# Turning sorted token tiles two at a time in the middle stage of a mixture-of-experts kernel

## The reference, cut to what matters

```python
rw = _gating(hidden_states, sim_matrix, gates)          # weights of the 16 experts, all but 1 or 2 of them 0
q = jnp.einsum('btc,ech,bte->bth', hidden_states, q_proj, rw)
k = jnp.einsum('btc,ech,bte->bth', hidden_states, k_proj, rw)
v = jnp.einsum('btc,ech,bte->bth', hidden_states, v_proj, rw)
scores = jnp.einsum('bqh,bkh->bqk', q, k) * scale        # then causal softmax over 128 tokens, ao = attn @ v
out = jnp.einsum('bth,ehc,bte->btc', ao, o_proj, rw)
```

## Time and profile before

| | |
|---|---|
| median of 3 runs | 1060.92 us (1060.51 to 1061.6) |
| profiled execution: span from first to last instruction | 1060.5 us |
| PE busy | 964.6 us, 91% of the span |
| DVE, ACT, POOL busy | 872.8, 581.5, 680.9 us |
| DMA | 137.72 MB, mean 130 GB/s |

### The profile page before, as it was taken

How to read it: one execution, slowest core, us unless ns; L and a number is a source line. 1 busy time by engine, 2 the same in 40 slices (tenths; PEclk the granted TensorE clock), 3 DMA queues, 4 the chain that set the end, 5 groups by cost and what they waited for, 6 DMA issues and landing times.

```text
span 1060.5 us, 23609 instructions
## 1 busy us (share of the span) xinstructions
PE 964.6 (91%) x6830; PEld 889.4 (84%) x6830; DVE 872.8 (82%) x2884; ACT 581.5 (55%) x1569; POOL 680.9 (64%) x896
## 2 busy tenths in 40 slices
PE   4999999999999639999999599999999999999998
PEld 3778887887788528999999499999999999998997
DVE  4799999999999747555555399999999999999998
ACT  4666666666666305444444355655555556555554
POOL 5447777777776683000000588888888888888885
PEclk9999999999999859999999699999999999999999
DMA  2123344443333257888886332333333233333231
GB/s 65 52 72 125 122 143 150 150 135 123 124 124 101 95 189 233 285 277 256 254 266 226 111 90 87 100 97 90 90 100 98 85 93 100 84 93 100 83 93 36
DMA packets 106308, 137.72 MB, mean 130 GB/s; under 512 B 13762, under 2 KB 93634, under 8 KB 106180
## 3 DMA queue, kind: packets, MB, share of 16 engines
q1 hardware_dynamic: 87348, 83.98, 25.2%
q0 software_dynamic: 17408, 50.35, 16.1%
q10 hardware_dynamic: 1424, 1.84, 0.5%
HBM read 70.06 MB, written 66.06 MB: 128 GB/s over the span
## 4 chain that ended last, share of the span: by engine, by line
DVE 44%; PE 36%; issue 10%; POOL 5%; ACT 2%; DMA 2%; SPq 1%; POOLq 0%; DVEq 0%; ACTq 0%
PE bank L1383 10%; PE bank L1385 9%; PE bank L1384 9%; DVE w_attn L1366 6%; DVE x L1320 4%; DVE qk_e L1320 4%; PE bank L1390 4%; DVE phi L1072 3%; DVE row_x L1360 3%; DVE attn L1084 2%; DVE kvm L1105 2%; POOL sorted_x L694 2%; DVE stats L1112 2%; DVE stats L957 2%; DVE zden L1081 1%
## 5 line engine op out<-in xcount | busy, mean ns | idle before, releaser
L1383 PE MATMUL bank<-wo_hi,split_lo 128*128 128x256 f32 x1024 | 304.8, 298 | 9.9 <-DVE x L1320 4.4
L1385 PE MATMUL bank<-wo_hi,split_hi 128*128 128x256 f32 x1024 | 289.0, 282 | 0.0
L1384 PE MATMUL bank<-wo_lo,split_hi 128*128 128x256 f32 x1024 | 288.7, 282 | 0.0
L1383 PEld LDWEIGHTS bank<-wo_hi,split_lo 128*128 128x128 f32 x1024 | 194.1, 190 | 23.1 <-DVE x L1320 11.3
L1384 PEld LDWEIGHTS bank<-wo_lo,split_hi 128*128 128x128 f32 x1024 | 194.3, 190 | 0.0
L1385 PEld LDWEIGHTS bank<-wo_hi,split_hi 128*128 128x128 f32 x1024 | 193.7, 189 | 0.0
L890 ACT ACTIVATE h<-bank,rwo 128x256 f32<-128x256 f32 x256 | 107.3, 470 | 117.9 <-PE bank L1385 113.9
L767 POOL DMA_INDIRECT row_y<-sorted_y,pair_now x128 | 124.2, 970 | 31.8 <-issue 18.3
L760 POOL COPY pair_now<-pair_at 128x2 uint32<-128x2 uint32 x64 | 16.0, 249 | 178.3 <-SPq L567 178.3
L1221 DVE TENSOR_TENSOR split_lo<-bank,split_hi 128x256 fp32r<-128x256 f32 x144 | 61.0, 424 | 69.1 <-ACT split_hi L852 67.8
L1320 DVE SCALAR_TENSOR_TENSOR x<-bank,rwo,x 128x256 f32<-128x256 f32 x256 | 108.5, 473 | 2.2 <-PE bank L1385 1.8
(11 more groups left out here) (215 smaller groups left out, 2630.5 us busy)
## 6 DMA issues: line engine op xcount, KB each, us to landing
sorted_y<-row_y SPq DMA_DIRECT2D x36, 384.0 KB, 3.2
sorted_y<-w_attn SPq DMA_DIRECT2D x36, 384.0 KB, 3.1
row_x<-sorted_x SPq DMA_DIRECT2D x72, 128.0 KB, 2.9
h_rows<-h SPq DMA_DIRECT2D x64, 128.0 KB, 1.7
row_x<-h_rows SPq DMA_DIRECT2D x64, 128.0 KB, 2.3
out_h<-row_x SPq DMA_DIRECT2D x64, 128.0 KB, 1.7
phi<-sorted_x SPq DMA_DIRECT2D x36, 128.0 KB, 3.0
qk_neg<-sorted_x SPq DMA_DIRECT2D x36, 128.0 KB, 3.1
```

The source lines that it names most:

```text
L1383: pe.matmul(ps, left[1][c], right[0][c], start=(c == 0), stop=False)
L1384: pe.matmul(ps, left[0][c], right[1][c], start=False, stop=False)
L1385: last = pe.matmul(ps, left[0][c], right[0][c], start=False, stop=(c == n - 1))
```

## The change

The turns, hi and lo of the middle stage are done for two tiles at once, at the even steps. Four transposes fill a whole PSUM bank of 512 columns, and hi and lo are one operation of 512 columns each. The eight split tensors become two large ones, so that the slots of two tiles lie next to each other. The products, the copies out, the loads and the stores stay operations of one tile (the stores of two), in their old order. The semaphores pair_turned, pair_hi and pair_lo count pairs of tiles in place of tiles; PE waits for the loads of both tiles ahead of the four transposes, and ACT, ahead of hi, for the product of the last tile that used the slots.

```diff
-        split = [[sb(f"split_{n}{q}", [P, CH, P], F32R) for n in ("hi", "lo")] for q in range(4)]
+        split_all = [sb(f"split_{n}", [P, 4, CH, P], F32R) for n in ("hi", "lo")]
+        split = [[w[:, q, :, :] for w in split_all] for q in range(4)]
+        split_pair = [[w[:, 2 * n:2 * n + 2, :, :].rearrange("p q c t -> p (q c t)") for w in split_all]
+                      for n in range(2)]
...
+        def after_two(eng, step, tile):
+
+            if tile.c >= 0:
+                eng.wait_ge(done[step], tile.c // 2 + 1)
...
-                        after(sp, "pair_turned", tile.shift(-8))
+                        after_two(sp, "pair_turned", tile.shift(-8))
...
-                    tile = i.shift(2)
-                    if tile.inside(PAIR_TILES):
-                        after(act, "pair_product", tile.shift(-4))
-                        after(act, "pair_turned", tile)
-                        act.copy(split[tile.q][0][:, :, :].rearrange("p c t -> p (c t)"),
-                                 ps_turn[tile.p][:, 0:C]).then_inc(done["pair_hi"], 1)
+                    first = i.shift(2)
+                    if first.inside(PAIR_TILES) and not first.p:
+                        after(act, "pair_product", first.shift(-3))
+                        after_two(act, "pair_turned", first)
+                        act.copy(split_pair[first.q // 2][0], ps_turn[first.q // 2][:, :]).then_inc(done["pair_hi"], 1)
...
-                    tile = i.shift(2)
-                    if tile.inside(PAIR_TILES):
-                        after(dve, "pair_hi", tile)
-                        hi, lo = [w[:, :, :].rearrange("p c t -> p (c t)") for w in split[tile.q]]
-                        dve.tensor_tensor(lo, ps_turn[tile.p][:, 0:C], hi.bitcast(F32), ALU.subtract
+                    first = i.shift(2)
+                    if first.inside(PAIR_TILES) and not first.p:
+                        after_two(dve, "pair_hi", first)
+                        hi, lo = split_pair[first.q // 2]
+                        dve.tensor_tensor(lo, ps_turn[first.q // 2][:, :], hi.bitcast(F32), ALU.subtract
...
-                    tile = i.shift(2)
-                    if tile.inside(PAIR_TILES):
-                        after(pe, "pair_lo", tile.shift(-2))
-                        pe.wait_ge(pair_loaded[tile.c % 8], tile.eighth * 16 + 16)
-                        turn(ps_turn[tile.p], *halves(x_buf[tile.c % 8])).then_inc(done["pair_turned"], 1)
+                    first = i.shift(2)
+                    if first.inside(PAIR_TILES) and not first.p:
+                        after_two(pe, "pair_lo", first.shift(-4))
+                        for tile in (first, first.shift(1)):
+                            pe.wait_ge(pair_loaded[tile.c % 8], tile.eighth * 16 + 16)
+                        turn(ps_turn[first.q // 2], *halves(x_buf[first.c % 8]), *halves(x_buf[first.c % 8 + 1])
+                             ).then_inc(done["pair_turned"], 1)
                     if i.inside(PAIR_TILES):
                         e = experts[i.q]
                         after(pe, "pair_copied", i.shift(-4))
-                        after(pe, "pair_lo", i)
+                        after_two(pe, "pair_lo", i)
```

## The result

The changed kernel takes 1062.70 us, the median of 20 runs, against 1061.04 us for the kernel before (20 runs): ratio 1.0017, 95% interval 1.0010 to 1.0023, 1.1 to 2.4 us slower. The forecast was 1060.0 us, 0.9 us faster.

What follows compares the result with a forecast made beforehand. PE was taken to bound the kernel from 441 us on. Terms -0.3 + 0 - 1.6 + 1.0 = -0.9 us gave a span of 1059.6 and a time of 1060.0 us; range 1058.8 to 1062.4.

Steps and rivals of the forecast that it cites:

- Start: Middle stage up to product 0: two more transposes come first, yet nothing is lost; 0.4 us if tile 3 is late.
- Steps 0 to 8: Where DVE's routing operations hold PE: 0.47 us lost waiting for lo in place of 2.05, so -1.6 us.
- Steps 8 to 30: During o_proj loads: DMAs may give gains back, odd tiles' loads are needed one product earlier; +1.0 us, bounds 0 and +3.5.
- The rival that more is kept: Pairs smooth the lo wait: 1.6 us kept whole, 0.5 or more of 3.22 us also gone; 1058.2 us, chance 0.17.
- The start of the o_proj loads at 408.4: The first o_proj load, held until DVE's first lo of o_proj, was to start near 408.4 us; before, 409.11.
- Steady stretch: PE's matmul work: a pair of tiles takes 2.545 us in place of 2.552; taken as -0.3 us.
- The rival of slow transposes: Four transposes in a row on PE cost 0.125 us each, +3.9 us; time 1064.2 us, chance 0.08.
- The ring of waits: Copies, hi and lo on ACT and DVE wait in a ring; 1063.1 us with late pairs, chance 0.13 for ring or late pairs.
- The clock: At the start, product 0 begins 0.45 us later; if PE's clock rises that much later too, 0.2 us is lost.
- the signs: Steady turns off 2.55 us by over 0.03, PE waiting there for lo, or tile 36 over 2 us from 443.0.

Runs made afterwards that it cites:

- e2: The changed kernel run again, unchanged, against the kernel before: ratio 1.0016.
- e1: The kernel before run again, unchanged: ratio 0.9999.
- e3: The kernel before with only the split tiles laid out as in the changed kernel: ratio 1.0000.
- e17: The changed kernel with each tile's turn behind its own load wait, in place of both waits ahead of four transposes: ratio 1.0008.
- e9: The kernel before with one o_proj piece loaded and split at every fourth step from step 8, in place of every step: ratio 0.9972.
- e10: The changed kernel with one o_proj piece loaded and split at every fourth step, in place of every step: ratio 0.9977.
- e6: The kernel before with 40 extra matmuls in PE's idle time ahead of the middle stage, to warm the engine: ratio 0.9993.
- e11: The kernel before with DVE's five routing operations at steps 26 to 42 in place of 0 to 4: ratio 0.9984.
- e5: The changed kernel with tiles 0 to 3 turned and split one at a time, pairs from tile 4 on: ratio 1.0004.
- e13: The changed kernel with tiles 0 to 3 single and o_proj at every fourth step: ratio 0.9972, median 1058.04 us.
- e14: The kernel before with o_proj at every fourth step, routing at steps 26 to 42 and 40 warming matmuls: ratio 0.9954, median 1055.75 us.

## Why the prediction was wrong

Two things were off in the same direction, and the size of a gain in the other. The figures are differences of the changed kernel and e2 from before, e1 and e3, by the table.

1. *Start: "Nothing is lost."* This step failed. Measured: +1.2 us to product 0, of which 0.43 is the additional turn, so +0.76 beside it; by e17 some 0.5 of it is the wait for tile 1's load, issued half a microsecond behind tile 0's. I had started both kernels at 391.17 us, the transpose of tile 0, and so put the later of the two first loads at nothing, without a reason; I put a price (0.4 us) only on tile 3. The rest of the step held: from the first transpose to product 0 I had 2.47 us, and it took 2.58. Product 0 to 4 differs by 0.05 us.

2. *Steps 0 to 8: -1.6 us.* Right in its mechanism, mis-sized. Lo of tiles 6 and 7 is what PE waits for, once, 0.58 us (0.47 forecast), and DVE's order ran as written. But the loss before, 2.05 us in the one profile that I had, was 1.2 to 2.1 in three: from 4 to 10 the kernel before takes 9.70, 8.85 and 9.51 us, the changed one 8.46 and 8.07. The gain is 1.1 us, and 0.9 us over all kernels with the routing operations in their old place. The profile that I had was of a slow execution: with 1.75 us between span and device time its 1060.5 us belong to a time of about 1062.2 (an estimate), over 1 us above the median.

3. *Steps 8 to 30: +1.0 us.* Right: 10 to 34 takes 1.1 us longer, and spreading o_proj in both kernels (e9, e10) takes 1.2 us out of their distance. The reason given, the odd tile's load needed one product earlier, fits the five waits, but no run tests it by itself. The other reason, that the loads give back what was gained before them, does not hold for single tiles: e6 and e11 reach product 10 1.9 and 1.3 us earlier after their first load than the kernel before (mean of three) and then take 32.96 and 33.29 us, no more than it does. The rival that more is kept falls with the 1.1 us. The start of the o_proj loads at 408.4 was wrong, since all ran 1 us later: 409.37.

4. *Steady stretch: -0.3 us*, by 2.545 us a pair. Right: 2.545 us, and 0.58 us less to the last product, of which 0.22 is the additional turn given back, so 0.36. The rival of slow transposes falls.

5. *The ring of waits.* From 441 us on PE never waits for lo, and from 405 to 434 us its waits name loads. It did not come. (Its lower bound of 2.53 us in the steps with o_proj is 0.09 below 2.21 + 0.41; nothing hung on that.)

6. *The clock.* It rises near 397.5 us in the changed kernel and near 398.5 in e2, against 396.1 to 396.8 in three profiles without pairs. The prediction had 0.2 us for it. With a warm engine the start's difference is unchanged, and at half clock product 0 to 4 takes about the same in both (6.28 to 6.81 against 6.31 to 6.60 us), so it explains nothing of the start's loss. Counted from the start of product 0, the clock rises after 3.1 us in the changed kernel and 4.3 in e2, against 3.0 to 3.8 in the three: no later by more than the profiles differ among themselves. By the Trainium skill ("TensorE: Matmul & The Clock Gate", Part 4) transposes do not count as PE work in the same way as other matmuls. A rise that keeps its distance from the first product, with eight transposes ahead of it in place of six, fits that but does not show it, since with the same six ahead the rise comes after 2.3 us in e5 and after 1.7 in e13. In the steady stretch, with transposes in it, the clock stays at 1.00.

The sum of the table's columns (mean of two profiles less mean of three): 1.19 + 0.05 - 1.09 + 1.07 - 0.58 = +0.64 us. The comparisons say 1.7 (1.1 to 2.4). Two things on record narrow the gap. With the four or five profiles on each side in which a stretch is as in the two kernels, in place of two and three, the columns give +1.22 - 0.16 - 0.90 + 1.32 - 0.58 = +0.90 us; and 0.2 us lies outside the span. That is 1.1 us, the lower end of the interval. What the other 0.6 us is stays open; a profiled execution varies by 1 us.

The weakest link was the sum itself: four terms of up to 1.6 us with both signs, each from one profile, for a result of 0.9 us. That the stretch from 441 us on would hardly change followed from PE's full row; the sign of the whole did not follow from anything I had. None of the signs came that the prediction named for being wrong: the pairs are 2.545 us apart, PE does not wait for lo in the steady stretch, and tile 36 is turned at 443.25 us, 0.25 from the 443.0 named. They watched the stage from its first transpose on, and the late first transpose, the step that failed, lies ahead of it.

## What to carry to other kernels

Larger operations bought nothing where their engines were half idle; look at what the grouping does to the waits instead. A group starts when its last input is there, so its first items wait for the last one's input. Here that cost where inputs arrived just in time: 1.2 us at the start of the stage and 1.1 to 1.3 under DMA contention. It cost nothing in the steady stretch, and where DVE held PE up, in the routing steps, it gained 0.9. Spreading side work (here o_proj's loads and the routing operations) over the idle steps behind it was worth more than the regrouping: 0.9972 and 0.9984 of the time by edits of one or two lines.

## What I had not expected of the hardware

Two profiled executions of one program (the kernel before and e1) differed by 1.1 us in a stage of 193 us: the two stretches that wait took 1.4 us less in e1, product 0 to 4, in which the clock rises, 0.3 us more, and the stretch without waits took 139.16 us in three profiles out of three. A warm engine did not show what its clock promised: e6 reached product 4 1.9 us earlier than the kernel before by the mean of three profiles (9.26 against 11.1 us) and kept that to the end of the stage (190.73 against 193.1), yet its time is only 0.7 us lower, with an interval from 1.9 faster to 0.4 slower. In e14 the warm engine stands on top of two spreads whose ratios multiply to 0.9956; with it the ratio is 0.9954. Where the rest of the gain is, no run shows.
